# Latent attention in a fused four-layer kernel: weighted sums in 512 columns, the mask by TensorE, and more of the small work on GpSimd

## The reference

```python
cq = rms_norm(hidden_states @ w_qa.T, q_a_ln_w)                 # 192 query latents
q_nope, q_pe = split((cq @ w_qb.T).reshape(b, s, 16, 192))      # 16 heads
ckv = hidden_states @ w_kva.T                                   # 64 key/value latents, 64 rotary keys
k_pe = ckv[..., 64:] * cos + rotate_half(ckv[..., 64:]) * sin
ckv_l = rms_norm(ckv[..., :64], kv_a_ln_w)
scores = where(causal, -inf, q_full @ k_full.T * scale)
attn = softmax(scores)
out = (attn @ v).reshape(b, s, 16 * 128) @ w_o.T                # v = ckv_l @ w_kvb
```

## Time and profile before

| | |
|---|---|
| median of 3 runs | 1982.46 us (1981.31 to 1984.31) |
| the profiled execution | 1981.61 us; its span from first to last instruction 1979.8 us |
| busy share of the span | PE 93%, PEld 83%, DVE 75%, ACT 52%, POOL 42% |
| instructions | PE 12032, DVE 4074, ACT 2694, POOL 865 |
| mean granted TensorE clock | 0.979 of full speed |

### The profile page before, as it was taken

How to read it: one execution, slowest core, us unless ns; L and a number is a source line. 1 busy time by engine, 2 the same in 40 slices (tenths; PEclk the granted TensorE clock), 3 DMA queues, 4 the chain that set the end, 5 groups by cost and what they waited for, 6 DMA issues and landing times. The chain is left out here.

```text
span 1979.8 us, 35608 instructions
## 1 busy us (share of the span) xinstructions
PE 1842.4 (93%) x12032; PEld 1647.6 (83%) x12032; DVE 1483.6 (75%) x4074; ACT 1038.8 (52%) x2694; POOL 835.4 (42%) x865
## 2 busy tenths in 40 slices
PE   7999999999999999999799999999999999978980
PEld 5788888888888888888589999999999999967980
DVE  8978778787878785665477888888888888864436
ACT  5434333333333333333277777777777777734653
POOL 1222323222332220000144466666666666655775
PEclk9999999999999999999799999999999999999995
DMA  3201000010101005573100010000000000126867
GB/s 126 87 1 33 10 24 22 11 32 1 33 1 50 30 22 159 175 248 123 30 12 17 18 41 28 21 21 20 19 19 19 20 19 14 39 74 180 205 136 257
DMA packets 102003, 118.81 MB, mean 60 GB/s; under 512 B 12567, under 2 KB 93723, under 8 KB 101184
## 3 DMA queue, kind: packets, MB, share of 16 engines
q1 hardware_dynamic: 89104, 108.42, 17.1%
q0 software_dynamic: 12288, 8.11, 2.7%
q10 hardware_dynamic: 432, 0.02, 0.0%
HBM read 75.50 MB, written 57.10 MB: 67 GB/s over the span
## 5 line engine op out<-in xcount | busy, mean ns | idle before, releaser
L282 POOL TENSOR_TENSOR kept_q_rows<-kept_q_rows 128x512 f32<-128x512 f32 x128 | 203.6, 1591 | 526.5 <-DVE kept_q_rows L547 526.5
L1569 POOL TENSOR_TENSOR kept_raw<-kept_raw,mla_row_inv 128x512 f32<-128x512 f32 x192 | 199.6, 1039 | 258.5 <-DVE mla_row_inv L1916 257.2
L372 ACT ACTIVATE kept_q_rows<-rwkv_r 128x512 f32<-128x512 f32 x128 | 76.7, 600 | 399.0 <-DVE rwkv_o_low L468 396.3
L1728 ACT ACTIVATE kept_raw<-kept_raw,mla_least 128x256 f32<-128x256 f32 (+1 forms) x512 | 227.7, 446 | 74.7 <-DVE mla_least L1900 73.4
L1900 DVE CUSTOM_DVE_ANT_0 kept_raw<-mla_score,kept_mask 128x256 f32<-128x256 f32 (+1 forms) x512 | 156.8, 352 | 83.3 <-PE mla_score L2275 52.8
L532 DVE TENSOR_TENSOR kept_q_rows<-rwkv_v,kept_q_rows 128x512 f32<-128x512 f32 x128 | 88.0, 688 | 111.7 <-PE rwkv_v L583 108.6
L539 DVE TENSOR_TENSOR_SCAN rwkv_state<-rwkv_decay_w,kept_q_rows 128x256 f32<-128x256 f32 x256 | 166.5, 692 | 4.1
L1654 POOL DMA_INDIRECT slots<-mla_x_out,mla_slot_now x128 | 130.0, 1016 | 30.8 <-issue 24.2
L1744 ACT ACTIVATE mla_p_high<-mla_turn 128x512 fp32r<-128x512 f32 x192 | 114.0, 594 | 46.0 <-PE mla_turn L2283 44.6
L1910 DVE TENSOR_TENSOR mla_p_low<-mla_turn,mla_p_high 128x512 fp32r<-128x512 f32 x192 | 128.0, 667 | 0.6 <-ACT mla_p_high L1744 0.6
L2283 PE MATMUL mla_turn<-kept_ident,kept_raw 128*128 128x128 f32 x768 | 115.8, 273 | 8.8 <-DVE mla_p_low L1910 8.8
(11 more groups left out here) (487 smaller groups left out, 6283.7 us busy)
## 6 DMA issues: line engine op xcount, KB each, us to landing
kept_raw<-in_experts SPq DMA_DIRECT2D x27, 384.0 KB
kept_raw<-in_rkvo SPq DMA_DIRECT2D x16, 512.0 KB
moe_y_in<-sums SPq DMA_DIRECT2D x32, 256.0 KB, 4.8
sums<-ffn_empty SPq DMA_DIRECT2D x12, 512.0 KB
slots<-ffn_empty SPq DMA_DIRECT2D x16, 361.2 KB
moe_e_rows<-slots SPq DMA_DIRECT2D x31, 180.6 KB
kept_x_in<-x SPq DMA_DIRECT2D x18, 256.0 KB, 18.2
mla_x_res<-x SPq DMA_DIRECT2D x17, 256.0 KB
```

The lines of the kernel that those rows point to most:

```text
L282: nc.gpsimd.tensor_tensor(gate[:, c % 2, :], key[:, c % 2, :], gate[:, c % 2, :], ALU.mult).then_inc(gated_done, 1)
L1569: nc.gpsimd.tensor_tensor(unit, unit, row_inv[:, v % PR, 0:len(heads)].rearrange("p (h a) -> p h a", a=1) .to_broadcast([P, len(heads), ke ...
L1728: last = nc.scalar.activation(probs[:, v % PR, i * keys:(i + 1) * keys], masked[:, v % 2, i * keys:(i + 1) * keys], ACT.Exp, bias=least[:, ...
```

## The change

The change does nine things, all in the attention stage.

1. Weighted sums: `v_parts` holds the high value latents in columns 0 to 63 and the low ones in columns 64 to 127, once. One matmul gives the sums with the high latents in partitions 0 to 63 and those with the low ones in partitions 64 to 127, for all 512 columns of a group at once. A group takes 2 matmuls (tile 0) or 4 (tile 1) of 512 columns.
2. To add the halves, ScalarE copies the lower half out (`keep_low_sums`, 64 by 512), VectorE adds it to the upper half in two instructions (`add_sums`, 64 by 256 each), ScalarE makes the high part from that in the next slot (`sums_high`), and GpSimd the low part (`sums_low`, 128 by 256), where VectorE did it before.
3. Mask: in tile 0 one more matmul for each slot adds the mask to the score bank ahead of the scores (`ident_first` by `mask_first`, 512 columns in bf16). VectorE then takes the least score of a slot in one `tensor_reduce` instead of four masking instructions, ScalarE reads the scores in PSUM, and TensorE waits for the exponentials (not the mask) before it takes the bank again.
4. Latents: ScalarE copies the 320 raw latents out of PSUM (`lat_rows`) ahead of its squares. TensorE can take the bank again when the squares are done (`squared`), VectorE's `latent` reads the copy, and has three instructions instead of six.
5. The rotary keys move from VectorE to GpSimd (`rotate_key`, three instructions of 64 columns), and `transpose_k` waits for them.
6. GpSimd's order in a slot: `sums_low` first, `norm_rstd` ahead of `scale_probs`, and in slot 10 the four router steps that make membership ahead of `latent_rstd` and `rotate_key` (before: behind both inverse roots).
7. Values: one instruction each on ScalarE and VectorE instead of two; GpSimd's four zero fills at the start go away.
8. VectorE copies the identity and the mask to bf16 once at the start.
9. Shared expert in the last rounds: TensorE multiplies up of unit `u` ahead of the transposes of unit `u + 1`, and the output of unit `u - 1` behind them; VectorE makes `hidden` first.

```diff
+        lat_rows = s.sb("lat_rows", [P, 2, LATC])
...
-        v_part = both("v", [P, 2, 2, 2, 2 * KVL])
+        v_parts = s.sb("v", [P, 2, 2, 2 * KVL], F32R)
...
+        low_sum = s.sb("low_sum", [KVL, 2, 512])
+        o_whole = s.sb("o_whole", [P, 2, 2, P])
...
+        mask_first = s.sb("mask_first", [P, HG, P], BF16)
+        ident_first = s.sb("ident_first", [P, P], BF16)
...
-            for part in v_part:
-                for b in range(2):
-                    last = nc.gpsimd.memset(part[:, :, :, b, (1 - b) * KVL:(2 - b) * KVL].bitcast(F32), 0.0)
-            last.then_inc(v_zeroed, 1)
...
-                if isinstance(n, int) and 0 < n < 4:
-                    pool.wait_ge(lat_scaled, n)
+                if n > 0:
+                    pool.wait_ge(lat_done, n)
...
+            def rotate_key(n):
+
+                pool.wait_ge(squared, n + 1)
+                t, at = n % 2, QLR + KVL
+                raw = lat_rows[:, t, at:at + DR]
+                nc.gpsimd.tensor_tensor(k_turn[:, t, 0, :], raw, rk[:, 0, t, :], ALU.mult)
+                nc.gpsimd.tensor_tensor(k_turn[:, t, 1, :].rearrange("p (a d) -> p a d", a=2),
+                                        raw.rearrange("p (a d) -> p a d", a=2)[:, ::-1, :],
+                                        rk[:, 1, t, :].rearrange("p (a d) -> p a d", a=2), ALU.mult)\
+                    .then_inc(k_turned, 1)
+                pool.wait_ge(k_turned, n + 1)
+                nc.gpsimd.tensor_tensor(k_rows[:, t, KVL:], k_turn[:, t, 0, :], k_turn[:, t, 1, :], ALU.add)\
+                    .then_inc(k_roped, 1)
...
+            def sums_low(seq, v):
+                group, _, where = sums_of(seq, v)
+                pool.wait_ge(o_high, group + 1)
+                nc.gpsimd.tensor_tensor(o_part[1][where], o_whole[:, group % 2, :, :], o_part[0][where].bitcast(F32),
+                                        ALU.subtract).then_inc(o_low, 1)
...
                     route_pool(seq - 2, v)
+                m, of, vs = slot_before(seq, v, SUM_LAG + 2)
+                if m >= 0 and completes(vs):
+                    sums_low(of, vs)
+                if v == 10 and exists(seq - 1):
+                    norm_rstd(seq - 1)
                 if kind == "latent" and v == 9:
                     latent_rstd(n)
                 m, of, v1 = slot_before(seq, v, 1)
                 if m >= 0:
                     scale_probs(m, v1)
+                if kind == "latent" and v == 9:
+                    rotate_key(n)
+                if exists(seq - 2) and v == 10:
+                    route_pool(seq - 2, v)
                 if kind == "pe":
                     of, tile, c = n // 8, n % 8 // 4, n % 4 - 2
                     pool.wait_ge(turn_filled, TURN_AT[f"q{tile}", 3, of - 1] + 1)
                     rope_sum(4 * of + 2 * tile + c, tile, c)
                 if v == 10 and exists(seq + 2):
                     latent_rstd(2 * (seq + 2) + 1)
-                if v == 10 and exists(seq - 1):
-                    norm_rstd(seq - 1)
+                    rotate_key(2 * (seq + 2) + 1)
                 if 0 <= v - SCATTER_FROM < 2 * TOPK and exists(seq - 3):
                     scatter(seq - 3, v - SCATTER_FROM)
-                if exists(seq - 2) and v in (5, 10):
+                if exists(seq - 2) and v == 5:
                     route_pool(seq - 2, v)
                 if exists(seq - 3) and v == 0:
...
+                nc.scalar.activation(lat_rows[:, n % 2, :], ps[:, 0:LATC], ACT.Copy)
...
+                from_scores = score_ps[v % 2] if tile == 0 else masked[:, v % 2, :]
                 for i, h in enumerate(heads):
                     last = nc.scalar.activation(probs[:, v % PR, i * keys:(i + 1) * keys],
-                                                masked[:, v % 2, i * keys:(i + 1) * keys], ACT.Exp,
+                                                from_scores[:, i * keys:(i + 1) * keys], ACT.Exp,
...
+            def keep_low_sums(seq, v):
+                group, bank, _ = sums_of(seq, v)
+                act.wait_ge(summed, group + 1)
+                if group >= 2:
+                    act.wait_ge(o_added, group - 1)
+                nc.scalar.activation(low_sum[:, group % 2, :], bank[KVL:, :], ACT.Copy).then_inc(low_kept, 1)
+
             def sums_high(seq, v):
-                group, src, where = sums_of(seq, v)
-                act.wait_ge(summed, group + 1)
-                nc.scalar.activation(o_part[0][where], src, ACT.Copy).then_inc(o_high, 1)
+                group, _, where = sums_of(seq, v)
+                act.wait_ge(o_added, group + 1)
+                nc.scalar.activation(o_part[0][where], o_whole[:, group % 2, :, :], ACT.Copy).then_inc(o_high, 1)
...
+                m, of, vs = slot_before(seq, v, SUM_LAG + 2)
+                if m >= 0 and completes(vs):
+                    sums_high(of, vs)
...
-                    sums_high(of, vs)
+                    keep_low_sums(of, vs)
...
-            def latent(n, t, ps=proj_ps):
+            def latent(n, t):
 
                 dve.wait_ge(lat_rstd_done, n + 1)
-                wait_reuse(dve, lat_done, n, 2)
-                nc.vector.tensor_scalar(cq_rows[:, t, 0:QLR], ps[:, 0:QLR], lat_rstd[:, 0:1], None, ALU.mult)
-                nc.vector.tensor_scalar(cq_rows[:, t, QLR:], ps[:, P:QLR], lat_rstd[:, 0:1], None, ALU.mult)
-                nc.vector.scalar_tensor_tensor(k_rows[:, t, 0:KVL], ps[:, QLR:QLR + KVL], lat_rstd[:, 1:2],
-                                               lnkv[:, :], ALU.mult, ALU.mult)
-                at = QLR + KVL
-                nc.vector.tensor_tensor(k_turn[:, t, 0, :], ps[:, at:at + DR], rk[:, 0, t, :], ALU.mult)
-                nc.vector.tensor_tensor(k_turn[:, t, 1, :].rearrange("p (a d) -> p a d", a=2),
-                                        ps[:, at:at + DR].rearrange("p (a d) -> p a d", a=2)[:, ::-1, :],
-                                        rk[:, 1, t, :].rearrange("p (a d) -> p a d", a=2), ALU.mult)\
-                    .then_inc(lat_scaled, 1)
-                dve.wait_ge(lat_scaled, n + 1)
-                nc.vector.tensor_tensor(k_rows[:, t, KVL:], k_turn[:, t, 0, :], k_turn[:, t, 1, :], ALU.add)\
-                    .then_inc(lat_done, 1)
+                raw = lat_rows[:, t, :]
+                nc.vector.tensor_scalar(cq_rows[:, t, 0:QLR], raw[:, 0:QLR], lat_rstd[:, 0:1], None, ALU.mult)
+                nc.vector.tensor_scalar(cq_rows[:, t, QLR:], raw[:, P:QLR], lat_rstd[:, 0:1], None, ALU.mult)
+                nc.vector.scalar_tensor_tensor(k_rows[:, t, 0:KVL], raw[:, QLR:QLR + KVL], lat_rstd[:, 1:2],
+                                               lnkv[:, :], ALU.mult, ALU.mult).then_inc(lat_done, 1)
...
+                if tile == 0:
+                    nc.vector.tensor_reduce(least[:, v % 2, :], score_ps[v % 2][:, :].rearrange("p (h k) -> p h k", h=HG),
+                                            axis=AX.X, op=ALU.min).then_inc(masked_done, 1)
+                    return
...
+            def add_sums(seq, v):
+                group, bank, _ = sums_of(seq, v)
+                dve.wait_ge(low_kept, group + 1)
+                if group >= 2:
+                    dve.wait_ge(o_low, group - 1)
+                high = bank[0:KVL, :].rearrange("p (a b q) -> p a b q", a=2, b=2)
+                low = low_sum[:, group % 2, :].rearrange("p (a b q) -> p a b q", a=2, b=2)
+                for b in range(2):
+                    last = nc.vector.tensor_tensor(o_whole[b * KVL:(b + 1) * KVL, group % 2, :, :], high[:, :, b, :],
+                                                   low[:, :, b, :], ALU.add)
+                last.then_inc(o_added, 1)
...
-                if half is not None and half % 2 == 0 and half >= 2:
-                    add_shared(half // 2 - 1)
+                if half == 2 * EARLY:
+                    add_shared(EARLY - 1)
                 elif half is not None and half % 2 == 1:
+                    unit_hidden(half // 2)
                     if half // 2 + 1 < EARLY:
                         unit_low(half // 2 + 1)
-                    unit_hidden(half // 2)
+                    if half >= 3:
+                        add_shared(half // 2 - 1)
                     unit_hidden_low(half // 2)
...
                 pe.wait_ge(lat_done, 2 * seq + 2)
+                pe.wait_ge(k_roped, 2 * seq + 2)
...
-                wait_reuse(pe, masked_done, m, 2)
+                if m >= 2:
+                    pe.wait_ge(exp_done if heads_of((m - 2) % SLOTS)[0] == 0 else masked_done, m - 1)
+                if tile == 0:
+                    if m == 0:
+                        pe.wait_ge(mask_set, 1)
+                    nc.tensor.matmul(score_ps[v % 2][:, :], ident_first[:, :], mask_first[:, :, :], start=True, stop=False)
                 for i, h in enumerate(heads):
                     score = score_ps[v % 2][:, i * keys:(i + 1) * keys]
                     if tile == 0:
```

(25 more changed lines are left out.)

57 lines of the change are left out of this document (29 added, 28 removed).

## The result

The changed kernel took 2045.37 us (median of 4, 2042.81 to 2047.51), the kernel before 1983.19 on the same chip: a ratio of 1.031 (95% interval 1.030 to 1.032). I had forecast 1998, with 2016 as the upper end: slower, as said, but by four times as much. The profiled execution spans 2045.7 us, 65.9 more than before.

The account below looks back on a forecast made before the run. TensorE was taken to bound the kernel before (47.7 us a period), GpSimd's stretch after (49.6). Periods +20.9, other sequences -7, start +1, end -3 and clock +4 made +16 on 1981.6: 1998 us, range 1968 to 2016.

Parts of the forecast that it names:

- TensorE's saving: TensorE's own work in each sequence: fewer, wider sums against four mask matmuls, 1.9 to 2.5 us less, 1.9 taken.
- GpSimd's lateness: GpSimd's slots 3 to 10: 6.6 us more ahead of the second root, handover 1.9 later, period 47.7 to 49.6.
- E: Stretch from the second root's end to the next handover; 0.43 in hand and 0.52 for the shorter latent taken off.
- the idle time swallows 3.57: GpSimd's idle time from slot 3 to the second root takes 3.57 of 6.6 us; the root comes 3.0 later.
- the 40 that I left it: VectorE's work in a sequence: additions +3.3, masks about -2, shorter latents; it stays near 40 of 47.7 us.
- The third piece: Start of GpSimd's run in slot 3: about 0.15 us earlier, since the mask there is shorter.
- The clock: TensorE's clock after its handover pause: up to 1.7 us a period, 0.4 taken, +4 in all (0 to 19).
- The ends: Outside the eleven periods: sequences 0 to 2, 14 and 15 -7, start +1, end of the stage -3 us.
- keep up: Rival: GpSimd's root is not late and TensorE stays the pace; 1952 to 1962 us, chance 0.20.
- late by less: Rival: GpSimd late at cheapest prices, period 47.7 to 48.3, TensorE's saving lost; 1973 to 1981 us, chance 0.17.
- The clock's rival: Rival: the pause costs TensorE's clock at every handover, 1.7 us more a period; 2012 us, chance 0.13.

Follow-up runs that it names:

- run 4: Changed kernel with GpSimd's second inverse root first in slot 10, both rotate_key behind it, and the sums' low parts on VectorE: 2023.0 us.
- run 5: Kernel before with only GpSimd's new order in slot 10 (norm_rstd and membership ahead of the second root): 1997.2 us.
- run 7: Kernel before with only the masks of slots 0 to 3 changed (TensorE matmul, one VectorE reduction): 1992.9 us.
- run 14: Kernel before with only the latents changed (ScalarE copies them out, VectorE scales from SBUF, GpSimd makes both rotate_key): 1997.5 us.
- run 3: Changed kernel with nine extra mask matmuls that nobody reads, filling TensorE's pause before the cq transposes: 2027.6 us.
- run 6: Kernel before with only the new weighted sums of 512 columns and all that belongs to them: 2035.6 us.
- run 2: Changed kernel with the sums' low parts made by VectorE again, GpSimd's order in slot 10 as changed: 2046.1 us.
- run 11: Changed kernel, second root and cq transposes first; low parts of slots 8 and 9 behind first root, last scatter behind second, VectorE's weight sum behind probs_low: 2038.5 us.
- run 12: As run 11, with the first rotate_key directly behind the first root: 2033.9 us.
- run 1: Changed kernel with GpSimd's second inverse root again ahead of norm_rstd and the membership steps in slot 10: 2022.3 us.

## Why the prediction was wrong

**TensorE's saving** was right. Four sums of 512 columns take 1.02 us where twelve took 1.51, and slots 1 and 9, free of waits, went from 4.38 to 4.08 and from 3.02 to 2.52 us. With the clock up it is busy 45.6 us a sequence (run 4), the 45 that I named.

**GpSimd's lateness** was the right step, and mis-sized: I had +1.9 a period, and without the clock it is 51.21 - 47.72 = 3.5. Its prices were right (0.70, 1.0, 0.66 to 0.73, 1.5), E fell by the 0.95 that I took off (0.43 and 0.52), and run 5 came within 0.1 of what they give. What failed is the sentence that the idle time swallows 3.57. Of that, 0.72 is still there in slot 7, since it is a wait for VectorE, and VectorE comes later too. It has 43.5 us a sequence, and not the 40 that I left it: its additions cost the 3.3 forecast, but the masks gave back 0.9 instead of 2 (run 7), the latents nothing instead of twice 0.52 (run 14), and a router step of slot 3, `odds_sum`, takes 1.0 more. In slot 7 of sequence 5 TensorE itself waits 0.59 for it, a wait that the sum didn't have. And 0.25 of GpSimd's idle time is new, behind `rotate_key`.

The third piece had the wrong sign. I had GpSimd's run start 0.15 earlier; with the clock kept up (run 3) slot 3's scaling comes 15.99 us after the handover, where it was 15.45, and slot 7's 0.7 later (A), though TensorE starts slot 7 0.4 earlier (slots 0 to 6 take 26.54 us there, 26.98 before). In slot 3 of sequence 5 VectorE works without a gap from `odds_sum` to the inverse that releases GpSimd's scaling at 1255.24, and `odds_sum` ends only when GpSimd's low part has ended (last section):

```profile
1252.12 1.16 DVE L2008 TENSOR_SCALAR mla_odds_sum<-mla_odds 128x64 f32<-128x64 f32 x1
...
1255.00 0.16 DVE L1958 RECIPROCAL mla_row_inv<-mla_row_sum 128x4 f32<-128x4 f32 x1
```

```profile
1252.48 0.74 POOL L1594 TENSOR_TENSOR mla_o_low<-mla_o_whole,mla_o_high 128x256 fp32r<-128x256 f32 x1
```

From slot 2's scaling to slot 3's it is 4.07 us before, 5.08 in run 3 and 5.32 in run 6, but 4.12 in runs 2 and 4, which leave GpSimd no low parts. So this one step costs 1.0 us on the path. The three pieces, 0.72, 0.25 and 0.85 (0.7 later instead of 0.15 earlier), make up, within 0.2, the 1.6 between 1.9 and 3.5.

**The clock** was a rival's step, and is the second mis-sized term: I took 0.4 a period and priced the rival at 1.7 more; the granted clock fell at every handover, and run 3 shows 1.77. Against it I had held that TensorE works twice as much in this pause as in the one of the earlier trace rows; it fell all the same, though TensorE's longest single wait was 2.22 us. The Trainium skill's page "TensorE: Matmul & The Clock Gate", Part 1 (The HAM clock gate), says that idling brings the clock down; the windows above agree, as far as several short waits with work between them are idling, and it was the better guide than my argument from one pause.

**The ends** had the wrong sign. Outside the eleven periods I had -9. The first scores of sequence 0 come 0.6 later, sequences 0 to 2 take 2.0 more, sequence 14 2.7 more (1.0 with the clock kept up, run 3) and the stretch from sequence 15 on 3.3 more: +8.6. I had let TensorE's saving show wherever GpSimd has less to do. Run 6 shows that the new sums cost there too: alone they add 3.5 us in sequences 0 to 2, 1.5 in sequence 14, and 7.3 from the first scores of sequence 15 to the experts. Which wait makes it was not followed, so the cause of this part stays open.

Together: 11 x 3.5 + 11 x 1.77 + 8.6 = 66.6 (65.9 by the spans), where I had 20.9 + 4 - 9 = 16. The miss falls on the three almost evenly: 18 us on the lateness, 15 on the clock, 18 on the ends. By the Trainium skill's page "GPSIMD Engine Reference", section 4.1 (Engine selection), I had named 2005, for a dearer `sums_low`. At 0.74 against VectorE's 0.41 it is 1.8 times as slow, much as that rule has it; but this price was not what failed.

**The rivals.** GpSimd didn't keep up, nor was it late by less. The clock's rival was right in its mechanism, and too low at 2012 since it stood on the same delay. That its price came out, 1.7 for 1.77, was partly luck: it halved 3.3 us, while 6.8 us ran at half the clock, with TensorE waiting for part of them anyway.

## What to carry to other kernels

Idle time of an in-order engine isn't a store for new work: ask of each gap what ends it, and whether that comes later as well. Here one engine's gap was a wait for another that the same change had filled. Follow every wait in the loop that passes between the two engines (both roots, not the last alone), and when a forecast makes the busiest engine pause in each round, price the half-clock stretch in each round too. And run each part alone: four of five made this kernel slower, by 0.6 to 2.7%, and the fifth can't be told from no change, which the whole, with its parts that mend each other, would never have shown.

## What was not expected of the hardware

VectorE's first scaling of the latents, 128x192 from SBUF, took 1.10 us beside GpSimd's 512-column scaling and 0.37 beside `rotate_key`; from PSUM, before, 0.40. It ends 0.12 us behind GpSimd's instruction (1227.89 + 1.10 = 1228.99, and 1227.84 + 1.03 = 1228.87). Between runs 11 and 12 what stands beside it differs: 0.80 beside a 0.73 us low part, 0.39 beside `rotate_key`.

```profile
1278.00 0.80 DVE L1911 TENSOR_SCALAR mla_cq_rows<-mla_lat_rows,mla_lat_rstd 128x192 f32<-128x192 f32 x1 [0.47 <-POOL mla_lat_rstd L1556]
```

```profile
1274.52 0.39 DVE L1911 TENSOR_SCALAR mla_cq_rows<-mla_lat_rows,mla_lat_rstd 128x192 f32<-128x192 f32 x1 [0.46 <-POOL mla_lat_rstd L1556]
```

The same happens to the router's `odds_sum` in slot 3, 128x64 from SBUF. It took 0.20 us in the kernel before and in runs 5, 7 and 14; with GpSimd's low parts in the queue beside it 1.16, in the changed kernel and in run 6; and 0.32 where VectorE makes these (runs 2 and 4). Before, then after:

```profile
L1960 DVE TENSOR_SCALAR mla_odds_sum<-mla_odds x12: 195/195/196, 1142.9 to 1667.7; 128x64 f32<-128x64 f32 x12
```

```profile
L2008 DVE TENSOR_SCALAR mla_odds_sum<-mla_odds x11: 1156/1161/1323, 1146.0 to 1675.5; 128x64 f32<-128x64 f32 x11
```

So in these places VectorE is held up until the other's instruction ends. Not every instruction of GpSimd does it: in run 4 the second scaling took 0.32 beside `norm_rstd` (128x2), which ran for 0.68.

```profile
1286.00 0.32 DVE L1899 TENSOR_SCALAR mla_cq_rows<-mla_lat_rows,mla_lat_rstd 128x192 f32<-128x192 f32 x1
```

The page "SBUF — State Buffer" of the Trainium skill, section "SBUF: two separate sides", describes such a lock between the two engines, held for a whole instruction. The long durations agree; the 0.32 does not, and `odds_sum` began 0.36 ahead of the low part that it waited for (1252.12 and 1252.48, with a scatter of GpSimd's running until 1252.44), where the page has the first to start go first. In all it took some 1.7 us a sequence from VectorE here, 0.7 in the first latents and 1.0 in `odds_sum`, and no sum of single prices showed it.

The clock's falls follow no single wait: 0.49 and 0.91 us at the handover left it up (run 5), as did 1.61, 0.47 and 0.82 spread over slots 10 and 11 (run 4); 0.45, 1.94 and 0.34 brought it down in most periods of run 1, but not in all; and 0.46, 0.78, 2.22 and 0.45 did in every period of the changed kernel, for twice as long. No rule comes out of these runs.
